# Graph layer, edge stage: where the reciprocal root of the variance is computed

## The reference

```python
x = jnp.concatenate((hi, hj, d2), axis=-1)       # rows of h gathered by src and dst, edge weight
msg = jax.nn.silu(x @ mW1 + mb1)
msg = _layer_norm(msg, ln_g, ln_b)               # (x - mu) * rsqrt(var + LN_EPS) * g + b
msg = jax.nn.silu(msg @ mW2 + mb2)
agg = jax.ops.segment_sum(msg, ei, num_segments=h.shape[0])
```

## Time and profile before

| | us |
|---|---|
| median of three runs | 2489.0 |
| lowest and highest | 2488.66 and 2492.62 |
| the profiled execution | 2497.57 |
| its span | 2495.7 |

### The profile page before, as it was taken

The page is one execution under the profiler, slowest core; times in us unless marked ns, Lnnn a source line. Parts: engine busy times, 40 slices in busy tenths (PEclk is TensorE's granted clock), DMA queues, the critical chain, the costliest instruction groups (busy, mean ns, idle before and its releaser), DMA issues. The chain is left out here.

```text
span 2495.7 us, 53843 instructions
## 1 busy us (share of the span) xinstructions
PE 2122.2 (85%) x12779; PEld 1780.0 (71%) x12780; DVE 1983.1 (79%) x6842; ACT 1353.4 (54%) x2905; POOL 1040.8 (42%) x1023
## 2 busy tenths in 40 slices
PE   0666466625999999999999999999999999678998
PEld 0444255524888888888888888888888888555776
DVE  0745799955998999998998999998998999264980
ACT  0000411114887777787777777777777777212231
POOL 0500145545554555554555555555554553143010
PEclk9777687756999999999999999999999999888999
DMA  1100000012222222222222222222222222201000
GB/s 65 48 1 1 3 26 26 26 49 80 71 71 67 73 72 70 71 72 71 71 71 67 71 71 72 72 70 69 70 73 69 71 71 47 86 1 26 1 26 26
DMA packets 65679, 135.10 MB, mean 54 GB/s; under 512 B 20868, under 2 KB 36219, under 8 KB 65374
## 3 DMA queue, kind: packets, MB, share of 16 engines
q0 software_dynamic: 42016, 111.40, 15.7%
q1 hardware_dynamic: 22405, 22.18, 2.9%
q10 hardware_dynamic: 1206, 0.83, 0.1%
HBM read 124.20 MB, written 10.16 MB: 54 GB/s over the span
## 5 line engine op out<-in xcount | busy, mean ns | idle before, releaser
L767 POOL DMA_INDIRECT g_rows<-b_table,idx_pair x834 | 795.8, 954 | 739.6 <-DVE idx_pair L907 582.4
L877 PE MATMUL ps<-w2g,nT 128*128 128x256 f32 x3336 | 790.5, 380 | 0.0
L877 PEld LDWEIGHTS ps<-w2g,nT 128*128 128x128 f32 x3336 | 602.2, 190 | 64.9
L792 ACT ACTIVATE normed<-act,shift,rstd_e 128x255 f32<-128x255 f32 x834 | 454.1, 597 | 210.4 <-DVE shift L979 206.9
L916 DVE TENSOR_TENSOR agg<-psG,agg 125x256 f32 x834 | 350.1, 420 | 122.8 <-PE psG L860 70.8
L860 PE MATMUL psG<-msg,ohf 128*125 128x256 f32 x1668 | 429.3, 380 | 0.1
L1013 DVE TENSOR_TENSOR g_rows<-psH,g_rows 128x512 f32<-128x512 f32 x417 | 285.5, 685 | 35.0 <-remote 14.9
L1020 DVE BATCH_NORM_STATS2 stat_e<-act 128x6 f32<-128x256 f32 x834 | 310.7, 415 | 0.0
L813 ACT ACTIVATE nT<-psM 128x512 f32<-128x512 f32 x417 | 249.3, 598 | 112.0 <-PE psM L869 95.4
L851 PE MATMUL psH<-a_sb,ohT 128*128 x1668 | 304.7, 305 | 0.0
L860 PEld LDWEIGHTS psG<-msg,ohf 128*125 128x125 f32 x1668 | 283.3, 187 | 26.2 <-issue 0.9
(11 more groups left out here) (194 smaller groups left out, 2562.2 us busy)
## 6 DMA issues: line engine op xcount, KB each, us to landing
g_rows<-b_table,idx_pair POOLq DMA_INDIRECT x834
h_sb<-in_x SPq DMA_DIRECT2D x1, 3125.0 KB
b_table<-b_out SPq DMA_DIRECT2D x25, 125.0 KB
x_sb<-in_x SPq DMA_DIRECT2D x1, 3125.0 KB
out<-x_sb SPq DMA_DIRECT2D x5, 625.0 KB
rec_d<-rec SPq DMA_DIRECT2D x1, 1668.0 KB, 6.6
agg<-rec_d SPq DMA_DIRECT2D x6, 256.0 KB, 4.8
row<-score_d SPq DMA_DIRECT2D x1, 1525.9 KB
```

Of the source, the lines that this page charges most:

```text
L767: pool.indirect_dma_start(g_rows[:, j, n, :], None, b_table[:, :], bass.IndirectOffsetOnAxis(ap=idx_pair[:, j, n:n + 1], axis=0)).then_inc ...
L792: ins = nc.scalar.activation(normed[:, (j - 9) % 2, n, 0:D - 1], act1[:, (j - 9) % RING, n, 0:D - 1], ACT.Identity, scale=rstd_e[:, 1 - fa ...
L877: mm = pe.matmul(ps2[:, k, n, :], nT[:, k, n, q, :], w2g[:, q, :], start=(q == 0), stop=(q == 1))
```

## The change

After step 5, VectorE's part ends: of the sixteen steps it keeps the five that give v, the variance times 256, and they stand where they stood (second slot of the group). Steps 6 to 16 are gone from VectorE. POOL does the rest in four operations, `root`, behind its two gathers of the slot in which ScalarE normalizes the group's first pair (j % 3 == 0): v / 256 + epsilon, its power by exph (a tile of -0.5), the mean times that, and times -0.5. It waits for the fifth step (s_var) and, before each operation, for its own last one (s_root). VectorE's first step of a group waits for s_rstd of the group before the last instead of for ScalarE's normalization of it.

```diff
--- before.py
+++ after.py
@@ -39,8 +39,6 @@
 TOPK = int(0.5 * NODES) - 1
 LN_EPS = 1e-5
 MAGIC = 12582912.0
-SEED = 1595932665.0
-K1, K2 = 0.703952253, 2.38924456
 assert NODES == NB * BLOCKS and 0 < TAIL <= EC and (COLS * P + BLOCKS * (WIN - 1)) // WIN <= P
 MAGIC_W, MAGIC_P = MAGIC * WIN, MAGIC * P
 
@@ -707,7 +705,8 @@
             s_hid = sem("s_hid")
             s_act1 = sem("s_act1")
             s_bn = sem("s_bn")
-            s_newton = sem("s_newton")
+            s_var = sem("s_var")
+            s_root = sem("s_root")
             s_rstd = sem("s_rstd")
             s_norm = sem("s_norm")
             s_nx = sem("s_nx")
@@ -758,7 +757,22 @@
             @block.gpsimd
             def _(pool):
 
-                def slot(t, j):
+                def root(d, j):
+                    g, par = (2 * d - 3, 1) if j < 3 else (2 * d - 2, 0)
+                    mean2, v, ve, y = tmp[:, 1, :], tmp[:, 4, :], tmp[:, 5, :], tmp[:, 6, :]
+                    r = rstd_e[:, par, :]
+                    pool.wait_ge(s_var, 5 * g + 5)
+                    pool.sem_inc(s_apart_pool, 1)
+                    pool.tensor_scalar(ve, v, 1.0 / D, LN_EPS, ALU.mult, ALU.add).then_inc(s_root, 1)
+                    pool.wait_ge(s_root, 3 * g + 1)
+                    pool.tensor_tensor(r, ve, exph[:, 0:6], ALU.pow).then_inc(s_root, 1)
+                    pool.wait_ge(s_root, 3 * g + 2)
+                    pool.tensor_tensor(y, mean2, r, ALU.mult).then_inc(s_root, 1)
+                    pool.wait_ge(s_root, 3 * g + 3)
+                    pool.sem_inc(s_apart_pool, 1)
+                    pool.tensor_scalar(shift[:, par, :], y, -0.5, None, ALU.mult).then_inc(s_rstd, 1)
+
+                def slot(t, d, j):
                     if has(t, 0):
                         need(pool, s_act1, t - RING + 1)
                         pool.wait_ge(s_idx, t + 1)
@@ -767,10 +781,12 @@
                             pool.indirect_dma_start(
                                 g_rows[:, j, n, :], None, b_table[:, :],
                                 bass.IndirectOffsetOnAxis(ap=idx_pair[:, j, n:n + 1], axis=0)).then_inc(s_gather[j], 16)
+                    if j % 3 == 0 and has(t, 9):
+                        root(d, j)
 
                 def body(d):
                     for j in range(RING):
-                        slot(d * RING + j, j)
+                        slot(d * RING + j, d, j)
 
                 pool.memset(agg_all[:, :], 0.0).then_inc(s_clear, 1)
                 pool.memset(normed[:, :, :, D - 1:D], 1.0).then_inc(s_one, 1)
@@ -915,74 +931,33 @@
                     need(dve, s_agg, 2 * t - 28 + n)
                     V.tensor_tensor(room, psG[0:NB, j % 2, n, :], room, ALU.add).then_inc(s_agg, 1)
 
-                def newton(t, d, j, n):
-                    if not has(t, 7 + (n > 8)) or j % 3 != 1 + (n > 8):
+                def variance(t, d, j, n):
+                    if not has(t, 7) or j % 3 != 1 or n > 5:
                         return
                     g, par = (2 * d - 2, 0) if j < 3 else (2 * d - 1, 1)
                     m0, m1 = stat[:, par, :, 0, 1], stat[:, par, :, 1, 1]
                     q0, q1 = stat[:, par, :, 0, 2], stat[:, par, :, 1, 2]
-                    delta, mean2, moment, square = tmp[:, 0, :], tmp[:, 1, :], tmp[:, 2, :], tmp[:, 3, :]
-                    v, ve, y, poly = tmp[:, 4, :], tmp[:, 5, :], tmp[:, 6, :], tmp[:, 7, :]
-                    r = rstd_e[:, par, :]
-                    done = g * 15
+                    delta, mean2, moment, square, v = (tmp[:, k, :] for k in range(5))
+                    done = g * 5
                     if n == 1:
                         dve.wait_ge(s_bn, 3 * g + 3)
-                        need(dve, s_norm, 3 * g - 3)
-                        V.tensor_tensor(delta, m0, m1, ALU.subtract).then_inc(s_newton, 1)
+                        need(dve, s_rstd, g)
+                        V.tensor_tensor(delta, m0, m1, ALU.subtract).then_inc(s_var, 1)
                     elif n == 2:
-                        V.tensor_tensor(mean2, m0, m1, ALU.add).then_inc(s_newton, 1)
+                        V.tensor_tensor(mean2, m0, m1, ALU.add).then_inc(s_var, 1)
                     elif n == 3:
-                        V.tensor_tensor(moment, q0, q1, ALU.add).then_inc(s_newton, 1)
+                        V.tensor_tensor(moment, q0, q1, ALU.add).then_inc(s_var, 1)
                     elif n == 4:
-                        dve.wait_ge(s_newton, done + 3)
+                        dve.wait_ge(s_var, done + 3)
                         V.scalar_tensor_tensor(out=square, in0=delta, scalar=D / 4.0, in1=delta, op0=ALU.mult,
-                                               op1=ALU.mult).then_inc(s_newton, 1)
-                    elif n == 5:
-                        dve.wait_ge(s_newton, done + 4)
-                        V.tensor_tensor(v, square, moment, ALU.add).then_inc(s_newton, 1)
-                    elif n == 6:
-                        dve.wait_ge(s_newton, done + 5)
-                        V.tensor_scalar(ve, v, 1.0 / D, LN_EPS, ALU.mult, ALU.add).then_inc(s_newton, 1)
-                    elif n == 7:
-                        dve.wait_ge(s_newton, done + 6)
-                        V.tensor_scalar(y.bitcast(I32), ve.bitcast(I32), -0.5, SEED, ALU.mult,
-                                        ALU.add).then_inc(s_newton, 1)
...
-                    elif n == 15:
-                        dve.wait_ge(s_newton, done + 14)
-                        V.scalar_tensor_tensor(out=r, in0=poly, scalar=-1.875 * K1, in1=square, op0=ALU.add,
-                                               op1=ALU.mult).then_inc(s_newton, 1)
+                                               op1=ALU.mult).then_inc(s_var, 1)
                     else:
-                        dve.wait_ge(s_newton, done + 15)
-                        V.scalar_tensor_tensor(out=shift[:, par, :], in0=mean2, scalar=-0.5, in1=r, op0=ALU.mult,
-                                               op1=ALU.mult).then_inc(s_rstd, 1)
+                        dve.wait_ge(s_var, done + 4)
+                        V.tensor_tensor(v, square, moment, ALU.add).then_inc(s_var, 1)
 
                 def slot(t, d, j):
                     def step(n):
-                        newton(t, d, j, n)
-                        newton(t, d, j, n + 8)
+                        variance(t, d, j, n)
 
                     if has(t, LAST):
                         add(t, j, 0)
```

23 lines of the change are left out of this document (removed).

## The result

On the chip of the first comparison the kernel before took 2488.83 us (median of 4 runs), the changed one 2609.95 us (4 runs, 2604.13 to 2617.64): a ratio of 1.0485, 95% interval 1.0452 to 1.0519. That is 122 us above the forecast of 2487.5 and 80 us beyond the upper end of the range. It isn't the whole result: on two other chips the same kernel is only 0.3% slower. So the loss has two parts with two causes. The profiled execution took 2606.1 us, its span is 2604.2.

What follows compares the result with a forecast made beforehand. TensorE's own work was taken to bound the edge stage. Terms 0 for the loop, 0 for shift and -1.5 us for the filling took the median 2489.0 to 2487.5 us; range 2480 to 2530.

Steps and rivals of the forecast that it cites:

- What bounds the kernel: Edge stage: TensorE paces it by its own work, 3.668 us a slot, with 6.3 us of waits in 1440 us.
- Removed from VectorE: 1.1 us a group: Edge loop: eleven small steps fewer per three slots, 153 us of VectorE's time, 0 on the path, hidden behind TensorE.
- down from 91% to about 75%: Expected sign in the loop: VectorE's busy share falls this far, with waits for psH or psG in its place.
- Added to POOL: a root of 2.2 us: Behind every third slot's gathers: four operations on 128x6, the power 1.36 us, each wait on its own result 0.08.
- POOL's load: Edge loop, per group of three slots: 6.7 us rises to 9.2 of 11.0 us, so the root fits.
- So it starts about 1 us later than now: The next slot's gather, queued behind the root: about 1 us later, covered by four slots (14.7 us) against 2.2 needed.
- When shift is ready: ScalarE's normalization every third slot: shift comes 0.4 us earlier; the root may be 0.9 us longer before TensorE stands; path 0.
- The filling: a gain of 1.5 us: Pipeline's filling: the first shift comes earlier, cutting TensorE's 2.13 us idle; gain 0 to 2.1 us, 1.5 taken.
- a later stall: Pipeline's filling: a subsequent stall may swallow the gain, hence its lower limit of 0.
- Rival A: Edge stage: POOL's power and VectorE's ohb, idx_pair or ohf collide on shared SBUF ports; 2522 us, at most 2551; 25 in 100.
- Rival B: Edge loop and filling: freed VectorE's slack of 1.15 us per group absorbs hiccups; 2482 us; 25 in 100.
- Rival C: Edge loop: root operations each cost 0.4 us more, shift is late, TensorE waits for msg; 2585 us; 4 in 100.

Runs made afterwards that it cites:

- three pairs together: Kernel before, only the gathers of three pairs issued together, six back to back every third slot: ratio 1.1374 on a holding chip; 2464.68 to 2470.23 us elsewhere.
- third series: Runs on one chip without holds: changed kernel against the kernel before (2466.73 us), 2476.67 us, ratio 1.0036; with filling roots moved a slot earlier, 2475.57 us.
- power-only kernel: Changed kernel with only the power on POOL, epsilon and shift back on VectorE: 2470.91 and 2471.44 us, ratios 1.0023 and 1.0022 to the kernel before, without holds.
- fifth series: Runs on one chip without holds, kernel before 2465.18 us: only the power on POOL, 2471.44 us; kernel before plus POOL's root on scratch, 2469.88 us.
- fourth series: Runs on one chip that holds increments: changed kernel against the kernel before (2489.11 us), 2606.83 us; with its first three roots on VectorE, 2610.24 us.

## Why the prediction was wrong

*What bounds the kernel.* Right: TensorE, 3.667 us a slot. What I took for its natural pace, 3.668, is just that; the 6.3 us of waits were mostly the visible end of holds: of the 11.1 us by which 15 slots between 30 and 400 are longer, 9.6 lie beside increments over 0.8 us late. In the same view I passed over four rows on "remote", 24 us together over ScalarE and VectorE.

*Removed from VectorE: 1.1 us a group.* Mis-sized, without consequence. On chips without holds VectorE's busy time per 1000 us is 849.67 in the changed kernel and 917.32 with all sixteen steps (three pairs together): 67.65 x 11.0 / 1000 = 0.74 us a group. The sign "down from 91% to about 75%" reckoned with 0.16 us for each of the eleven steps, 1.76 in all, against the 1.1 of the sum; the share became 85%. That it buys nothing was right.

*Added to POOL: a root of 2.2 us.* Close. The power takes 1.36 us alone, as the slope gave it; the whole root lasts 587.24 to 589.64 = 2.40 us in the filling and 1305.11 to 1307.65 = 2.54 in the loop, where VectorE's ohf runs beside it. The last operation costs 0.24 and waits 0.20, not 0.08.

*POOL's load, "from 6.7 us to 9.2 us of 11.0. It fits."* **Here the prediction failed, and in the step behind it.** The sum left out the 0.30 us between one pair and the next: 0.95 + 0.30 is spent on every gather, 2.50 on a pair, 7.5 us on a group. The root takes the time from 1305.04, where the last gather ends, to 1308.30, less the usual 0.30: 2.96. POOL has 10.5 us to do in 11.0, and its waits say so. The group of its gathers in the changed kernel, third series:

```profile
L781 POOL DMA_INDIRECT g_rows<-b_table,idx_pair x834 | 819.6, 983 | 333.5 <-issue 282.3 <-DVE idx_pair L923 42.6 <-ACT act L820 8.4
```

Before (first trace) POOL waited 582 us for idx_pair; here 43. It no longer follows VectorE, it works off a backlog, so gathers come four to six in a row. By the prediction's own 2.5 us for root and gap, POOL would have been 1 us late, and the idle time ahead of the next pair (1.5 us) would have taken that up. The power-only kernel shows that case: it blocks POOL for 1.4 us a group, 8.9 of 11.0 in all, and its gathers stay in pairs.

*"So it starts about 1 us later than now", with four slots of slack.* True for the data, which are never late in the loop: on the two chips without holds on which the changed kernel was traced, its loop keeps 3.667 us. **The step priced only the latest moment of a gather and put what gathers in a row do to the other engines at nothing, without a row for it.** On the chips that hold increments that is 102 of the 108.5 us between the two spans of the first comparison. The kernel without a root, whose gathers were merely bunched, loses more.

*When shift is ready.* Right: ScalarE's idle time ahead of the normalization fell from 210.4 to 37.5 us, 24.5 in the third series, and it now ends on POOL.

*The filling: a gain of 1.5 us.* Right for the row that it was read from, wrong for the sum. On the chip of the first comparison the first normalization starts 30.96 us after the first transpose instead of 32.28, 1.3 us earlier, and slot 12 opens at 42.9 instead of 46.7 us. The prediction reckoned with "a later stall" that may swallow the gain; later stalls made a loss of it: slot 30 opens at 116.5 instead of 113.1. The row was itself the end of a hold. On chips without holds VectorE's steps are through earlier, POOL is still busy with the gathers of the first pairs when the variance is ready, and the loss is 5 to 8 us.

*Rival A.* The place was right, the loser wrong. VectorE's ohf lasts at most 453 ns and ohb at most 422 in all 417 slots of the first trace; the power is what stretches, from 1352 to 1551:

```profile
L768 POOL TENSOR_TENSOR rstd_e<-tmp,exph x139: 1352/1362/1551, 591.1 to 2226.3; 128x6 f32<-128x6 f32 x139
L980 DVE TENSOR_TENSOR ohf<-iota_n,rec x417: 404/412/453, 600.1 to 2246.4; 128x250 f32<-128x250 bf16 x139
```

The rule cited from the Trainium skill (SBUF — State Buffer, "SBUF: two separate sides"), a lock for a whole instruction, has the later one wait. At 1305.30 ohf was ahead of the power at 1305.39, and the power took 0.19 us longer, of which the first 0.32 lie beside ohf. These rows fit the rule in who gives way, not in a full wait: in all 63 such cases of the first trace the power took 1541 to 1551 ns. Where POOL was ahead, they don't fit it. In 128 of 139 groups of the power-only kernel (fifth series) ohf lies wholly inside the power and takes its 0.41 us, while the power takes 1.49 in the median:

```profile
1307.03 1.48 POOL L764 TENSOR_TENSOR rstd_e<-tmp,exph 128x6 f32<-128x6 f32 x1
...
1307.36 0.41 DVE L980 TENSOR_TENSOR ohf<-iota_n,rec 128x250 f32<-128x250 bf16 x1
```

No row shows VectorE locked out by the power, and there the measurement decides.

*Rival B* gave 2482 for the freed VectorE. It does run ahead now, and waits for TensorE's psH (134.1 us in the third series). Without a root at all the kernel took 2459.73 against 2469.39 us, one run each, so there may be something in B, but the change doesn't reach it. *Rival C*, the only one with a price near the result (2585 us), is out all the same: it had TensorE wait for msg, and that wait comes to 0.2 us in the whole trace.

## What to carry to other kernels

An engine that does small steps in time with another one has a budget per period; add every gap between its instructions, not only those inside a pair, before saying that something fits. Here POOL followed its feeder with 8.9 us of work in 11.0 and went in bursts with 10.5: look at what the bursts collide with, and at the filling, where the engine has a backlog already. And read the waits that end on "remote" in the trace of before; there they were the one sign of a cost that the change would multiply. And take a change of half a percent, or of five, to more than one chip before believing it.

## What the hardware showed

On two of the six occasions (the first comparison and the fourth series) TensorE's semaphore increments came late while POOL issued gathers back to back, from the third gather of a run on: median 2.8 and 4.4 us within the third and fourth gather of the runs of six. Of the increments that were over 1 us late in a run of six, some 85% arrived 1.0 to 1.8 us after the last gather had ended, most of the others while the run still went on. Behind pairs they are late as well, but little: in the first trace of the kernel before, 189 of 471 that end in the 1.3 us after a pair are over 0.1 us late, none over 0.7. In the filling, in a run of 18 gathers, they are up to 13 us late. Of VectorE's a few come up to 1.2 us late, in the last two gathers of a run of six or just behind; ScalarE's and POOL's are on time everywhere. On the four other occasions not one came over 0.02 us late in the loop, in runs of six or seven. The kernel before took 2488 to 2489 us on the first kind, 2465 to 2469 on the other. Whether this belongs to a chip or to a state that it is in, what in it holds the increments, and what runs of three or four cost on their own, these runs don't say.

A pair of gathers that waits for the pair before it to land makes the kernel POOL-bound at 4.82 us a slot: POOL stands for 2.5 to 2.6 us ahead of each pair, and the landing, not the issue, then sets the pace.
